# Attention in turns of eight key tiles instead of four, on one Trainium2 core

## What is computed

```python
q = (x @ Wq).reshape(b, s, HEADS, DIM_HEAD).transpose(0, 2, 1, 3)
k = (x @ Wk).reshape(b, s, HEADS, DIM_HEAD).transpose(0, 2, 1, 3)
v = (x @ Wv).reshape(b, s, HEADS, DIM_HEAD).transpose(0, 2, 1, 3)
scores = jnp.einsum('bhqd,bhkd->bhqk', q * scale, k * scale)
weights = jax.nn.softmax(scores.astype(jnp.float32), axis=-1).astype(scores.dtype)
out = jnp.einsum('bhqk,bhkd->bhqd', weights, v)
return out.transpose(0, 2, 1, 3).reshape(b, s, HEADS * DIM_HEAD) @ Wo
```

## Time and profile before

| | |
|---|---|
| median of 3 runs | 3453.54 us (3452.11 to 3456.22) |
| the profiled execution | 3454.07 us, its span 3452.3 us |
| PE busy | 3236.8 us, 94% of the span |
| POOL busy | 2698.8 us, 78% |
| DVE busy | 2336.9 us, 68% |
| ACT busy | 1977.5 us, 57% |
| attention_pairs | from 731 us to 3174 us of the span |

### The profile page before, as it was taken

The page is one execution under the profiler, slowest core; times in us unless marked ns, Lnnn a source line. Parts: engine busy times, 40 slices in busy tenths (PEclk is TensorE's granted clock), DMA queues, the critical chain, the costliest instruction groups (busy, mean ns, idle before and its releaser), DMA issues. The chain is left out here.

```text
span 3452.3 us, 58551 instructions
## 1 busy us (share of the span) xinstructions
PE 3236.8 (94%) x21507; PEld 2069.0 (60%) x21517; DVE 2336.9 (68%) x3762; ACT 1977.5 (57%) x3730; POOL 2698.8 (78%) x1332
## 2 busy tenths in 40 slices
PE   5896699389999999999999999999999999998998
PEld 2785288345555555555555555555555555555898
DVE  5787488676666666667666776667666666664664
ACT  3894499245555555555655565555555555555454
POOL 0782088049999999999999999999999999996333
PEclk9997799689999999999999999999999999999999
DMA  1330132110000000000000000000000000000000
GB/s 26 92 89 24 37 97 83 31 55 1 4 1 4 1 4 4 1 4 1 4 1 4 1 13 7 1 4 1 4 1 4 4 1 2 1 1 22 19 23 13
DMA packets 66063, 60.09 MB, mean 17 GB/s; under 512 B 7786, under 2 KB 49332, under 8 KB 65716
## 3 DMA queue, kind: packets, MB, share of 16 engines
q1 hardware_dynamic: 63970, 55.93, 5.6%
q10 hardware_dynamic: 1810, 0.37, 0.1%
HBM read 49.46 MB, written 6.82 MB: 16 GB/s over the span
## 5 line engine op out<-in xcount | busy, mean ns | idle before, releaser
L1521 POOL TENSOR_TENSOR den_g<-den_g,p 128x1024 f32<-128x1024 f32 x888 | 2115.8, 2383 | 143.5 <-ACT p L1443 24.3
L1596 DVE TENSOR_REDUCE quarters<-psum 128x1 f32<-128x512 f32 x2004 | 1290.6, 686 | 647.4 <-PE psum L972 602.9
L1443 ACT ACTIVATE p<-psum 128x512 f32<-128x512 f32 x2048 | 1084.1, 600 | 385.7 <-PE psum L1320 342.6
L1333 PE MATMUL psum<-p,v 128*64 128x512 f32 x4096 | 922.8, 592 | 0.0
L1333 PEld LDWEIGHTS psum<-p,v 128*64 128x64 f32 x4096 | 293.2, 137 | 582.0 <-issue 507.0
L972 PE MATMUL psum<-k_main,q_main 64*128 64x512 f32 x2048 | 449.8, 423 | 7.1 <-DVE quarters L979 5.8
L1320 PE MATMUL psum<-row_shift,row_ones 64*128 64x512 f32 x2048 | 417.8, 390 | 0.0
L1320 PE MATMUL psum<-q_main,k_rest 64*128 64x512 f32 x2048 | 416.6, 390 | 0.0
L1320 PE MATMUL psum<-q_main,k_main 64*128 64x512 f32 x2048 | 414.2, 391 | 2.2 <-PEq L1112 2.2
L1320 PE MATMUL psum<-q_rest,k_main 64*128 64x512 f32 x2048 | 416.1, 390 | 0.0
L972 PEld LDWEIGHTS psum<-k_main,q_main 64*128 64x128 f32 x2048 | 207.1, 184 | 196.4 <-issue 120.6
(11 more groups left out here) (284 smaller groups left out, 3283.2 us busy)
## 6 DMA issues: line engine op xcount, KB each, us to landing
work<-bc_rows SPq DMA_DIRECT2D x128, 256.0 KB, 3.1
resid<-in_resid SPq DMA_DIRECT2D x8, 256.0 KB, 3.9
x_mid<-resid SPq DMA_DIRECT2D x8, 256.0 KB, 2.6
residual<-x_mid SPq DMA_DIRECT2D x8, 256.0 KB, 4.4
x<-x_mid SPq DMA_DIRECT2D x8, 256.0 KB, 2.7
out<-mixed SPq DMA_DIRECT2D x8, 256.0 KB, 2.3
xa<-x_mid SPq DMA_DIRECT2D x4, 256.0 KB, 3.5
w_qkv<-in_Wq SPq DMA_DIRECT2D x16, 64.0 KB, 1.9
```

The costliest lines, as they stand in the source:

```text
L1333: last = nc.tensor.matmul(o_bank[hi(h), :], vv[:, kt, hi(h)], p[:, u % LIVE, h, :], start=(kt == 0), stop=(kt == KT - 1))
L1443: nc.scalar.activation(p[:, u % LIVE, h, :], bank_of["score", u, h], ACT.Exp, scale=float(DH) ** -0.5).then_inc(p_ready, 1)
L1521: nc.gpsimd.tensor_tensor(sums, first, src, ALU.add).then_inc(added_g, 1)
L1596: nc.vector.reduce_max(quarters[:, to % 2, h, n:n + 1], bank_of["max", u, h], X_AXIS).then_inc(max_read, 1)
```

## The change

- `TURN` is 8: two turns to a chunk. The first part of a turn makes the scores of 8 units and 8 maxima steps, at `MAX_AT` = 0, 4, 9, 13, 18, 23, 27, 32, which with the steps themselves are the slots 0, 5, 11, 16, 22, 28, 33 and 39 of 40. (In a turn of four they are 0, 6, 13 and 19 of 20.)
- Uses may stand between any two units of the second part: in turn 0 the projection "0" in front, "den" after 4 units, "values" after 6, "shift" behind; in turn 1 "out" in front and the projection "1" after 4 units.
- `AHEAD` is 8 instead of 6: the maxima run eight units ahead, the shift is made in turn 0, and `attention_first` does two steps more.
- `LIVE` is 12 instead of 10. The room comes from `residual`, which in attention_pairs now lies in the part of xaT of the first sequence and is loaded later (at pair 7), and in the last phase has a tile of its own.
- DVE adds the tiles 8 and 9 of each chunk (`SUMMED`, `add_pair`, line 1605 of the changed kernel) with one `reduce_sum` into den_v, and POOL adds that sum: 14 adds instead of 15. `add_pair` stands behind the use "den" in DVE's queue, in front of the maxima of turn 1.
- PE waits for a chunk's queries to be rounded before the first maxima step of a chunk of another pair.

```diff
-LIVE = 10
+LIVE = 12
-AHEAD = 6
+AHEAD = 8
-TURN = 4
+TURN = 8
-USES_AT = {(0, "before"): 0, (0, "behind"): "values", (1, "before"): "den", (2, "before"): "out",
-           (2, "behind"): "shift", (3, "before"): 1}
+USES_AT = {(0, 0): (0, "vector"), (0, 4): ("den", "vector"), (0, 6): ("values", "scalar"), (0, TURN): ("shift", "scalar"),
+           (1, 0): ("out", "vector"), (1, 4): (1, "vector")}
+SUMMED = (8, 9)
-MAX_AT = (0, 5, 11, 16)
+MAX_AT = (0, 4, 9, 13, 18, 23, 27, 32)
...
-    adds = KT - 1
+    adds = KT - 2
...
-                    for u in range(first, first + TURN):
-                        values(u)
-                    if (i, "behind") in at_turn:
-                        use(at_turn[i, "behind"])
+                    for place in PLACES:
+                        if (i, place) in at_turn:
+                            use(at_turn[i, place])
+                        if place < TURN:
+                            values(first + place)
...
-                    if kt == 0 or (g == GC - 1 and kt >= BY_VECTOR):
+                    if kt in (0, SUMMED[0]) or by_vector(g, kt):
                         continue
...
+                    if kt == SUMMED[1]:
+                        src = flat(pair_sum[:])
+                        pool.wait_ge(pair_done, g + 1)
...
+                def add_pair(g):
+
+                    at = g * KT + SUMMED[0]
+                    dve.wait_ge(p_ready, 2 * (at + 2))
+                    if g:
+
+                        dve.wait_ge(added_g, (g - 1) * adds + added_with(SUMMED[1]))
+                    two_tiles = p[:, at % LIVE:at % LIVE + 2].rearrange("p k h q -> p (h q) k")
+                    nc.vector.reduce_sum(flat(pair_sum[:]), two_tiles, X_AXIS).then_inc(pair_done, 1)
...
+                    if i % TURNS == 0 and not by_vector(g, SUMMED[0]):
+                        add_pair(g)
```

More of the change, by code:

```diff
@@ L1174, in hand_out_banks @@
             next(steps, None)
-        use(i, "before")
-        now += TURN * SUPPOSED["values"]
-        use(i, "behind")
+        for place in PLACES:
+            use(i, place)
+            if place < TURN:
+                now += SUPPOSED["values"]
     return bank_of, in_front
@@ L1266, in _ @@
                         sp.wait_ge(use_full, use_of[1, CHUNKS * pair - 1] + 1)
+                    if pair == PAIRS - 1:
+                        for c in range(CHUNKS):
+                            sp.dma_start(residual[:, c], tokens(x_in, 0, c)).then_inc(residual_loaded, 16)
                     for i, w in enumerate(("Wq", "Wk", "Wv")):
@@ L1337, in use @@
                 def use(k):
-                    what, g, _, _ = uses[k]
+                    what, g, *_ = uses[k]
                     bank = bank_of["use", k]
@@ L1610, in _ @@
                         make_shift(nc, st, quarters[:, (g + 1) % 2], maxima[:], shift).then_inc(shift_ready, 1)
+                    for k in uses_of(i):
+                        what, reader = uses[k][0], uses[k][4]
+                        if reader != "vector":
+                            continue
+                        if what == "out":
+                            add_outputs(k)
+                        elif what == "den":
+                            invert(k)
+                            normalise(k)
+                        else:
+                            take_rest(k)
+                    if i % TURNS == 0 and not by_vector(g, SUMMED[0]):
+                        add_pair(g)
                     if i % TURNS == 0 and g in job_at:
@@ L1618, in _ @@
                                 st.link(nc.vector.tensor_tensor(flat(den_v[:]), first, flat(p[:, u % LIVE]), ALU.add))
-                dve.wait_ge(freed_by_vector, sum(place == "before" for *_, place in uses))
+                dve.wait_ge(freed_by_vector, sum(reader == "vector" for *_, reader in uses))
         nc.all_engine_barrier(sems_to_clear=sem_range(su.sems))
```

91 lines of the change are left out of this document (48 added, 43 removed).

## The result

The changed kernel takes **3546.48 us** (median of four runs, 3543.42 to 3549.74); the kernel before took 3453.65 beside it (3452.11 to 3456.22). The ratio is **1.0272**, 95% interval 1.0259 to 1.0285: slower by 93 us. The profiled execution has a span of 3544.7 us against 3452.3. The forecast was 3511 with a range of 3413 to 3550.

What follows compares the result with a forecast made beforehand. PE was taken to set the pace, POOL close behind. Per chunk -0.66 + 0.45 + 0.95 = +0.74 us, over 62 chunks +46; with +10, +2.3 and -0.3 that is +58 on 3454.07: 3511 us, range 3413 to 3550.

Steps and rivals of the forecast that it cites:

- turn 1, slot 6: PE at slot 6 of turn 1 waits for a maxima bank that late DVE returns: a stall of 0.56 us.
- turn 1, tight places: Later in turn 1 DVE stays close behind PE; the tight places cost 0.4 us more.
- Turns of eight, -0.66: PE's attention chunk: two changeovers fewer at 0.33 us each, 0.66 us saved, if uses among the values cost as in front.
- Tighter maxima, +0.45: Turn 0 on PE: maxima banks wanted again before they are back; 0.45 us a chunk, bounds 0.1 and 0.7.
- DVE late for turn 1, +0.95: DVE does add_pair after normalising, so turn 1's maxima start late and PE stalls 0.95 us, bounds 0.5 and 1.2.
- Price of the sum, 2.29: DVE's add_pair takes 2.29 us, as a reduce over neighbours in memory does; upper bound 4.57.
- rival 3: The strided sum on DVE costs as if read twice, 4.57 us: about 3630, 3570 if half as bad; chance 0.20.
- Statistics, 8 x 1.3: In 8 chunks DVE's token statistics behind add_pair add 1.3 us each to turn 1's delay: +10 us.
- the new add on DVE buys PE nothing: POOL's 14 adds instead of 15: without the pair sum POOL would just not bind, so no gain for PE.
- +2.3 for two more steps in attention_first: Two more steps in attention_first, bound by DVE at 1.13 us each: +2.3 us.
- Rival 1: Banks come back in time: five-slot loops cost nothing, late DVE under 0.3 us; about 3420 us, chance 0.18.
- Rival 2: Even: only half of the stalls come about, 0.6 us a chunk; 3460 us, chance 0.12.

Runs made afterwards that it cites:

- e5: Changed kernel with maxima read over half of each bank's columns and tiles 8 and 9 summed in front of the den operations: 3420.6 us, ratio 0.9904.
- e1: Changed kernel with one move: DVE sums tiles 8 and 9 in front of the three den operations instead of behind them: 3488.3 us, ratio 1.0106.
- e2: Changed kernel without the sum of two tiles on DVE; POOL makes 15 adds a chunk again: 3491.5 us, ratio 1.0108.
- e6: Changed kernel with respaced maxima and their bank table, no sum on DVE, fifteen adds on POOL: 3442.7 us, ratio 0.9967.
- e3: Changed kernel with the sum in front of the den operations, maxima at slots 0, 5, 10, 15, 21, 27, 33, 39 and another bank table: 3438.4 us.
- e7: Changed kernel with the early sum, maxima nearer the front (slots 0, 5, 10, 15, 20, 26, 32, 38) and another bank table: 3448.5 us, ratio 0.9983.
- e8: Changed kernel with only the respaced maxima and their bank table; the sum stays behind the den operations: 3509.3 us, ratio 1.0155.
- e4: Changed kernel with each maximum read over 256 of its bank's 512 columns, the sum still late: 3464.0 us, ratio 1.0032.

## Why the prediction came out as it did

Per chunk, by the prediction's own steps:

| step | forecast | measured |
|---|---|---|
| two times 40 slots without waits | 18.74 | not seen alone; taken as forecast |
| rest of the two turns | 18.87 | 18.56 (9.83 + 8.73) |
| turn 0, tighter maxima | +0.45 | +0.81 (slots 10.18 for 9.37) |
| turn 1, slot 6 | +0.56 | +0.76 |
| turn 1, tight places | +0.4 | +0.73 (slots 10.86 for 9.37, less 0.76) |
| chunk | 39.0 | 39.6 |

- **Turns of eight, -0.66: the saving came, and was larger by 0.31.** By the first two rows of the table a chunk without waits is 37.30, where I had 37.61. The uses among the values cost less than outside them: "den" 0.86 (1300.56 to 1301.42) where I put 0.91, "values" 0.88 and "1" 0.86 where I put 0.97. That e5's chunk of 37.8 lies so near 37.61 is in part luck, since 0.45 of waits is still in it. (The stretch that I called a chunk in the earlier trace rows begins with a turn 1, as the "den" in the earlier trace rows shows; its length is that of a chunk all the same.)
- **Tighter maxima, +0.45: this term failed, by 0.36 in turn 0 and 0.33 in turn 1.** The loop itself was nearly right: the maximum at slot 11 starts on PE at 1288.73, DVE at 1289.27, its first read ends 0.69 later, and slot 16 starts at 1290.11, 0.16 behind the slot's due time where I had 0.14. By the medians turn 0 comes late by 0.06 at slot 11, 0.16 at 16, 0.05 at 30 and 0.06 at 35: 0.33 together, less than the 0.55 I had added up. What I did not have is the restart: behind a step that waited, the next comes 0.31 later and not 0.23 (1290.11 to 1290.42). It stands behind slots 11, 16, 30, 33 and 35, five times 0.08 = 0.40, and the remaining 0.08 is spread thin. The sum had no term for it. The reason I gave for taking 0.45 and not 0.55, half arrays that run a little apart, has nothing to stand on: the program waits for both heads' banks before the first matmul of a step. So a short wait costs 0.08 more than its length, and the upper bound of 0.7 was too low.
- **DVE late for turn 1, +0.95: the mechanism and the slot were right, the size too small.** DVE was free at 1.53 and not at 1.2. 0.22 of this is a gap between the normalising and the sum, 0.06 the sum's 2.35 for 2.29. At the other end the step from the end of the read to the matmul took 0.05 instead of 0.15 (the read that starts at 1307.58 ends at 1308.25, and slot 6 starts at 1308.30), while at slot 16 of turn 0 it took 0.15; what makes the difference was not tried. Slot 6 thus lost 0.76; 1.49 in the whole turn stand against an upper bound of 1.2.
- **Price of the sum, 2.29 for operands 4 KB apart: right.** It took 2.35 at the median of 63, and 2.31 in e1. The Trainium skill's rule of a penalty for each new line (SBUF — State Buffer, Specifications), which gave rival 3 its place, is worth at most 3% in this instruction. Rival 3 (3570 to 3630) falls.
- **Statistics, 8 x 1.3: right**, 8 x 1.16 = 9. What I did not have is the granted clock, which fell behind the stop in two of the eight: 3 us.
- **POOL, "the new add on DVE buys PE nothing": right** for the chunks: e2 is as long as e1 and e6's chunk as long as e3's. It waits 3.9 us in each chunk for DVE's sum, and no wait of PE follows. At the end of attention it does bring about 4 us (e3 against e6), where I had 0 within 3. The +2.3 for two more steps in attention_first can't be told from the traces: the second chunk begins between 3.7 us earlier and 4.3 later in the nine of them than in the kernel before.
- **Rival 1**, banks back in time, falls: the five-slot loops are paid for. Its 3420 is what e5 reaches, 3421, but only with half reads and the early sum. **Rival 2**, 3460, falls too: the stalls were bigger than forecast, not half.

The signs: a stop of half a microsecond or more in front of slot 6, ended by the maxima, came (0.59); the sum right behind the normalising, with its end over 1 us into turn 1, came (1.60); POOL's one gap in each chunk came; the turns were 20.0 and 19.6, where I had 19.8 and 19.2. The error of 35 us is that of the chunk, 62 x 0.6 = 37: waits larger by 0.89 than forecast (55 us), and the rest of the turns shorter by 0.31 (19 us). That the time lies in the range at all is thus partly luck: with the rest of the turns as forecast it would have been about 3565, above 3550.

## What to carry to other kernels

When a change lengthens the turns of a loop, look at what stood in an engine's idle time before: here one instruction of 2.35 us, once a chunk, on an engine that was busy for 69% of the span cost 58 us by standing behind the last operation of a turn instead of in the 3.6 us gap in front of it, and nothing once moved. For buffers handed back and forth, work out the loop for the later of the two that a step waits for, grant no slack that no row shows, and add the restart of the waiting engine; then move the slots apart where the loop is tight and hand out the banks anew, which together was worth another 50 us. Such a table is to be measured: the one of e7 looked looser and was slower. Such waits are to be read from the differences of starts, since the modelled ends hide them.

## What the runs showed of the hardware

- Behind a step that had waited for a bank, the next step of two matmuls started 0.31 us later, where it is 0.23 in a row without waits. It did so even where the wait itself was under 0.03 (slot 11 of turn 0 in e3: on time, and slot 12 comes 0.30 behind it).
- The late sum started 0.22 us behind the end of DVE's own normalising (14.5 us in 62 chunks, 0.59 in two of them). The program has two waits there, one for the end of that normalising itself (line 1585) and one for the weights (line 1603), and they stand in the trace 0.04 and 0.15 behind its end. In its early place, where DVE still worked on what stood in front while the queue went through the sum's own waits, the same instruction shows no gap. Neither wait was taken out by itself.
- A sum over pairs of numbers that lie 4 KB apart took 2.35 us for 2048 numbers a row; over neighbours it was 2.29.
- An add of DVE with both operands in SBUF took 1.22 us alone and 3.26 to 3.30 while POOL made an add of the same size; POOL's took 3.15 to 3.19 then instead of 2.38 (e6 twice, the kernel before once). The sum of two tiles on DVE, which reads one operand, showed nothing of the kind: 2.31 us beside POOL's adds in e1, where these took 2.36.
- In all eight chunks with statistics PE was idle for 1.76 to 1.77 us in front of slot 6. Behind that the granted clock fell to 0.50 in two of the eight in the changed kernel and in four in e8, each time for 3.4 us, with 0.43 us a step instead of 0.23: 1.4 us lost each time. In e4, where PE was idle for 1.5 us there, it fell in none.
